# A graph kernel's edge tables moved from its first pass into LSTM pass 2, with a new load order and new orders in pass 1's last tiles

## The reference, cut to what matters

```
h = relu(adj @ (x @ Wg0 + bg0));  h = relu(adj @ (h @ Wg1 + bg1))
for p in 1..4:   # windows of p steps; the last step of each window is replaced
    h[:, last of window] = last state of LSTM_p over the window (p steps)
x = layernorm(x + h)
# graph attention over E = 256 edges (src, dst)
Xq, Xv = x @ W_lin.T, x @ W_val.T
e = sum_d a * leaky_relu(Xq[src] + Xq[dst]) + log(adj[src, dst] + 1e-8)
attn = softmax of e over the edges of one src;  Y[src] += attn * Xv[dst]
x = layernorm(x + Y @ W_out.T)
```

## Time and profile before

| | |
|---|---|
| median of 3 runs | 907.78 us (907.5 to 908.27) |
| profiled execution | 907.49 us, of which its span 905.4 us |
| TensorE busy | 873.8 us, 97% |
| VectorE busy | 696.4 us, 77% |
| ScalarE busy | 610.9 us, 67% |
| GpSimd busy | 176.9 us, 20% |
| granted TensorE clock, mean | 0.998 |

### The profile page before, as it was taken

How to read it: one execution, slowest core, us unless ns; L and a number is a source line. 1 busy time by engine, 2 the same in 40 slices (tenths; PEclk the granted TensorE clock), 3 DMA queues, 4 the chain that set the end, 5 groups by cost and what they waited for, 6 DMA issues and landing times.

```text
span 905.4 us, 15427 instructions
## 1 busy us (share of the span) xinstructions
PE 873.8 (97%) x5411; PEld 759.5 (84%) x5411; DVE 696.4 (77%) x1570; ACT 610.9 (67%) x1113; POOL 176.9 (20%) x500
## 2 busy tenths in 40 slices
PE   7999999999999999999999999999998999999796
PEld 6888888877787779999998887878887888987685
DVE  5777777777778788777787677777987887886786
ACT  2677777777767667677676666666886777776254
POOL 0000000000000000000000000113564465555665
PEclk9999999999999999999999999999999999999999
DMA  4211221001000000000000086777073010111123
GB/s 112 82 47 56 63 59 47 25 1 47 1 1 0 1 1 1 1 1 1 2 1 1 0 176 151 162 166 184 2 159 75 25 37 24 37 37 36 48 59 82
DMA packets 43275, 45.44 MB, mean 50 GB/s; under 512 B 2592, under 2 KB 40128, under 8 KB 40128
## 3 DMA queue, kind: packets, MB, share of 16 engines
q1 hardware_dynamic: 39520, 27.47, 10.5%
q0 software_dynamic: 2304, 16.78, 9.1%
q10 hardware_dynamic: 1376, 0.22, 0.1%
HBM read 19.29 MB, written 8.39 MB: 31 GB/s over the span
## 4 chain that ended last, share of the span: by engine, by line
PE 85%; DVE 8%; issue 3%; ACT 3%; DMA 1%; ACTq 0%; POOL 0%; POOLq 0%; DVEq 0%
PE psum L446 8%; PE psum L447 8%; PE psum L448 8%; PE psum L464 6%; PE psum L460 6%; PE psum L461 6%; PE psum L1174 6%; PE psum L1101 6%; PE psum L364 3%; PE psum L382 3%; PE psum L392 3%; PE psum L1185 2%; PE psum L1157 2%; PE psum L355 2%; PE psum L354 2%
## 5 line engine op out<-in xcount | busy, mean ns | idle before, releaser
L564 ACT ACTIVATE work<-psum,bias 128x512 f32<-128x512 f32 (+1 forms) x408 | 233.3, 623 | 29.1 <-PE psum L464 28.5
L446 PE MATMUL psum<-hT_hi,w_hi 128*128 128x512 f32 (+1 forms) x408 | 148.7, 365 | 3.3 <-ACT work L564 2.6
L447 PE MATMUL psum<-hT_lo,w_hi 128*128 128x512 f32 (+1 forms) x408 | 147.3, 361 | 0.0
L448 PE MATMUL psum<-hT_hi,w_lo 128*128 128x512 f32 (+1 forms) x408 | 147.2, 361 | 0.0
L548 ACT ACTIVATE work<-work 128x512 f32<-128x512 f32 (+1 forms) x112 | 63.9, 570 | 102.1 <-DVE work L819 70.8
L1009 POOL DMA_DIRECT2D hT_lo<-hT_hi x8 | 7.3, 918 | 556.1 <-DVE hT_lo L794 536.9
L828 DVE TENSOR_TENSOR work<-work 128x512 f32<-128x512 f32 (+1 forms) x111 | 67.9, 611 | 54.1 <-ACT work L548 54.1
L460 PE MATMUL psum<-hs_hi,w_hi 128*128 128x512 f32 (+1 forms) x288 | 103.8, 360 | 0.8 <-DVE hs_hi L792 0.7
L464 PE MATMUL psum<-hs_lo,w_hi 128*128 128x512 f32 (+1 forms) x288 | 104.4, 363 | 0.0
L461 PE MATMUL psum<-hs_hi,w_lo 128*128 128x512 f32 (+1 forms) x288 | 103.2, 358 | 0.0
L446 PEld LDWEIGHTS psum<-hT_hi,w_hi 128*128 128x128 f32 x408 | 76.8, 188 | 17.4 <-ACT work L564 5.4
(11 more groups left out here) (206 smaller groups left out, 1862.8 us busy)
## 6 DMA issues: line engine op xcount, KB each, us to landing
work<-x SPq DMA_DIRECT2D x32, 256.0 KB, 3.0
x_stage<-x_by_feature SPq DMA_DIRECT2D x8, 1024.0 KB, 5.6
hT_lo<-hT_hi POOLq DMA_DIRECT2D x8, 1024.0 KB, 9.7
hT_lo<-x_stage POOLq DMA_DIRECT2D x8, 1024.0 KB, 7.0
out<-x_kept SPq DMA_DIRECT2D x31, 256.0 KB, 2.3
work<-L_gnn_Wih SPq DMA_DIRECT2D x4, 256.0 KB, 3.1
work<-L_gnn_Whh SPq DMA_DIRECT2D x3, 256.0 KB, 3.0
out<-x_kept SPq DMA_DIRECT2D x2, 128.0 KB, 2.3
```

The source lines that it names most:

```text
L446: pe.matmul(out, w_hi[:, w, g, :], xh, start=True, stop=False)
L447: pe.matmul(out, w_hi[:, w, g, :], xl, start=False, stop=False)
L448: mm = pe.matmul(out, w_lo[:, w, g, :], xh, start=False, stop=(t == 0))
L564: op = act.activation(gate[s][g][:, 0:ph.width], psum[:, 4 * s + g, 0:ph.width], ACT.Tanh if g == G else ACT.Sigmoid, bias=bias[:, b:b + 1])
```

## The change: what it does

1. **Loads.** `adj` goes to ScalarE's queue as its first, with `bg0` and `Wg0`. SP issues x of tiles 0, 1, 2 at once, then the weights, and the edges' lists and `a` last. ScalarE runs a one-column copy (`first_act`) after its first three loads, and issues the other five after that.
2. **Ones multiplied at first.** TensorE makes five f32 products of the tile `ones` as soon as that is filled, before it waits for `adj`, and one more after the transposition. The `degrees` and `rank_rows` products move one slot later, the biases' transposition to slot 3.
3. **Edge tables.** They leave pass 1. On VectorE they are cut into thirteen pieces, most of them at the head of one item of pass 2 (`edge_numbers` at j = 1, `edge_keys` 3, `rank_edges` 5, `permutes` 7, `sorted_cols` 8, `sorted_rows` 12, `row_edges` 13, `edge_ends` 15, `adjacent` 16, `sames` 17, `signs` 19, `caps` 21), the last two in pass 3. TensorE makes its parts at the head of items 8, 12 and 16 of pass 2 and item 6 of pass 3, in the free F bank. The logarithm follows item 2 of pass 3.
4. **One-pass products.** `permute` and `spread` are f32r, so the four products of 256 columns are f32r products. The other sorting products stay f32.
5. **Attention weights.** Their transposition moves from slot 3 to slot 7, their centring to slot 6, their copies to slot 8.
6. **Pass 1's last tiles.** From slot 34 on ScalarE reads gate O before it makes the tanh, and VectorE makes the cell before it cuts the state of the tile before. In slot 36, TensorE makes gates I and G of pass 2's first item between gates G and O of tile 31 (`first_input`), in the idle banks of the layers.

The diff, cut to the places that matter here:

```diff
+
+    SORT_COLS, SORT_ROWS, ADJACENT = 8, 12, 16
+    LOG_AT, DIAG_AT, LOG_ROWS_AT = 2, 4, 6
...
+    permute = sb("permute", [P, EC, E], F32R)
+    spread = sb("spread", [P, 2, EC, P], F32R)
     sorted_col = sb("sorted_col", [P, EC, 2])
     adj_edge = sb("adj_edge", [P, EC])
...
 
-        sp.dma_start(adj_sb[:, :], adj).then_inc(S["adj_loaded"], 16)
         load_x(0)
-        sp.dma_start(wg0[:, :], Wg0).then_inc(S["wg0_loaded"], 16)
-        sp.dma_start(edge_row_i[:, :], src.rearrange("(a e) -> a e", a=1).broadcast_to([P, E])).then_inc(S["rows_loaded"], 16)
         load_x(1)
+        load_x(2)
         load_piece(0)
         for j, w in enumerate((W_lin, W_val, W_out)):
             sp.dma_start(w_raw[1][:, j, :], w).then_inc(raw_loaded[1], 16)
-        load_x(2)
+        sp.dma_start(edge_row_i[:, :], src.rearrange("(a e) -> a e", a=1).broadcast_to([P, E])).then_inc(S["rows_loaded"], 16)
+        for j, e in enumerate((src, dst)):
+            sp.dma_start(edge_col_i[:, j, :], e.rearrange("(c p) -> p c", p=P), allow_slow_non_contiguous=True).then_inc(S["cols_loaded"], 16)
+        sp.wait_ge(S["a_zero"], 1)
+        for h in range(HEADS):
+            sp.dma_start(T.a_wide[h * DH:(h + 1) * DH, T.a_col + h:T.a_col + h + 1], a[h].rearrange("(d o) -> d o", o=1),
+                         allow_slow_non_contiguous=True).then_inc(S["a_loaded"], 16)
         for n in range(SLOTS):
...
+        def sort_cols():
             pe.wait_ge(S["permutes"], EC)
+            for r in range(EC):
+                for c in range(EC):
+                    mm = pe.matmul(psum[:, F, 2 * r:2 * r + 2], permute[:, c, r * P:(r + 1) * P].bitcast(F32), edge_col[:, c, :],
+                                   start=(c == 0), stop=(c == EC - 1))
+            mm.then_inc(S["cols_psum"], 1)
+
+        def sort_rows():
             pe.wait_ge(S["spreads"], 2 * EC)
-            pe.wait_ge(S["degree_ready"], 2)
             for j in range(2):
...
+        def first_input(g, bank, free):
+
+            assert bank == g
+            ph = phases[1]
...
+            xh, xl = windows_at(ph, hi_bt, 0, 0, 0), windows_at(ph, lo_bt, 0, 0, 0)
+            w, out = piece_of[1, 0], psum[:, bank, 0:ph.width]
+            pe.wait_ge(S["w_lo_ready"], len(pieces))
+            pe.matmul(out, w_hi[:, w, g, :], xh, start=True, stop=False)
+            pe.matmul(out, w_hi[:, w, g, :], xl, start=False, stop=False)
+            pe.matmul(out, w_lo[:, w, g, :], xh, start=False, stop=True).then_inc(gate_psum[g], 1)
 
         def slot(n):
...
                 mm.then_inc(S["ah_psum"], 1)
+            if n - 5 == tiles - 1:
+                first_input(I, AX, S["axT_ready"])
+                first_input(G, AH, S["ahT_ready"])
             if has(n - 5):
...
+        def run_warm(count):
+
+            for _ in range(count):
+                pe.matmul(psum[:, GATE_BANK[O], 0:P], ones[:, :], ones[:, :], start=True, stop=True)
+
+        pe.wait_ge(S["consts"], 1)
+        run_warm(5)
         pe.wait_ge(S["adj_loaded"], 16)
         pe.wait_ge(S["ident_ready"], 1)
         pe.transpose(psum[:, SIDE, 0:P], adj_sb[:, :], ident[:, :]).then_inc(S["adjT_psum"], 1)
-        degrees()
+        run_warm(1)
+        pe.wait_ge(S["adjT_ready"], 1)
         for n in range(SLOTS):
             slot(n)
             if n == 0:
+                degrees()
+            elif n == 1:
                 rank_rows()
-            elif n == 1:
-                sort_edges()
-            elif n == 2:
...
+                    if ph is phases[1]:
+                        if j in (SORT_COLS, SORT_ROWS, ADJACENT):
+                            assert t == 0 and k % 2 == 0
+                            pe.wait_ge(S["gates_read"], ph.items_before + j + (CREDIT - 1))
+                        if j == SORT_COLS:
+                            sort_cols()
+                        elif j == SORT_COLS + 2:
...
     def run_scalar(act, entry):
+        act.dma_start(adj_sb[:, :], adj).then_inc(S["adj_loaded"], 16)
         act.dma_start(bg0_all[:, :], bg0.rearrange("(a h) -> a h", a=1).broadcast_to([P, P])).then_inc(S["bg0_loaded"], 16)
-        for j, e in enumerate((src, dst)):
-            act.dma_start(edge_col_i[:, j, :], e.rearrange("(c p) -> p c", p=P), allow_slow_non_contiguous=True).then_inc(S["cols_loaded"], 16)
+        act.dma_start(wg0[:, :], Wg0).then_inc(S["wg0_loaded"], 16)
...
+                ended = not has(n - 2)
+                if ended:
+                    gate_of(O, k)
...
                         tanh_of(k)
+                    if ph is phases[2] and it == 0 and k == LOG_AT:
+                        act.wait_ge(S["eps_done"], 1)
+                        act.activation(log_adj[:, :], adj_edge[:, :], ACT.Ln).then_inc(S["log_done"], 1)
...
+
+            ended = not has(n - 2)
+            if ended and has(n - 5):
+                cell_product(n - 5)
             if has(n - 6):
-                k = n - 6
...
                             entry.scale_query(dve)
+                    j = it * ph.per_iter + k
+                    if ph is phases[1]:
+                        if j == 1:
+                            edge_numbers()
+                        elif j == 3:
+                            edge_keys()
+                        elif j == 5:
+                            rank_edges()
+                        elif j == SORT_COLS - 1:
+                            permutes()
+                        elif j == SORT_COLS:
+                            sorted_cols()
...
+                        log_rows()
                     if t > 0:
                         dve.wait_ge(S["f_ready"], nf)
```

197 lines of the change are left out of this document (120 added, 77 removed).

## The result

The changed kernel takes 902.4 us (median of 5 runs, 901.25 to 903.26); the kernel before, run beside it, takes 907.78 (5 runs, 907.48 to 908.83). The ratio is 0.9941, 95% interval 0.9928 to 0.9954: faster by 0.6%. The forecast was 899.9, with a range of 896.4 to 903.8. The sign and the range hold, and the gain is 5.4 us where 7.85 were forecast.

The account below looks back on a forecast made before the run. TensorE, busy 97% of the span, was taken as the bound. Start -9.0, `log_to_rows` -0.45, weights +0.3, end of pass 1 -2.8, edge tables +4.1 sum to -7.85 from 907.49; plus 0.3 to the median: 899.9 us, range 896.4 to 903.8.

Parts of the forecast that it names:

- The start: Stretch before slot 5: new loads, ones and tables moved out start slot 5 at 20.6 instead of 29.55, -9.0 us.
- the slow work: First blocks at the start: products slow until TensorE has worked without pause; 0.2 us, or 0.9 more per first two blocks.
- The worse case for `bg1`: Rank rows at the start: taken as in time, with up to 2 us of waiting if `bg1` lands at 11.3.
- `log_to_rows` and the weights' turning: Pass 1: moving `log_to_rows` out gives 0.45 us; turning the attention's weights in slot 7 puts 0.3 back.
- The end of pass 1: Last tiles: four waits for ScalarE, 2.81 us together, mostly go by reading gate O first; -2.8, bounds -1.4 and -3.4.
- Pass 2: Edge pieces delay VectorE's chain, which TensorE pays: +1.3 us at item 8, +1.7 at items 12 to 16.
- the waits of 0.5 for the low half: Sign in pass 2: TensorE waits for `hs_lo` of items 8 and 16, about 0.5 us each.
- Pass 3: The logarithm's table loads make item 3's state 0.5 us late; with `log_rows` and diagonals 0.6, +1.1.
- A: Rival, passes 2 and 3: VectorE's pieces are hidden, only TensorE's 2.2 us is paid; 898.0 us, chance 0.20.
- C: Rival, pass 3: the logarithm's switches stall ScalarE 5.5 us instead of 2.8, the extra reaching TensorE; 902.6, chance 0.05.
- B: Rival, start: x lands late and work stays slow through two tiles, slot 5 at 24.0; 903.3 us, chance 0.20.
- D: Slower rival, passes 2 to 4: one chain, each edge piece delays it wholly, 14.1 us; 909.9 us, chance 0.04.

Follow-up runs that it names:

- `bg1` early: The kernel with the logarithm in pass 4, with `Wg1` and `bg1` issued by SyncE between x of tiles 1 and 2; 898.45 us.
- The run with the pieces behind the cell: The kernel with the ones filled up, with `sorted_cols`, `adjacent`, `log_rows` behind the item's cell and TensorE's wait for them ahead of gate F, made last; 899.99 us.
- The run with tables in pass 1: The kernel before with the new loads, ones and end of pass 1, but tables, their f32 products and attention weights at their old places; 904.85 us.
- the ones filled up: The changed kernel with seven ones instead of five ahead of `adj` and two more ahead of the degrees; 901.32 us.
- the old end of pass 1: The changed kernel with the orders of pass 1's last tiles as in the kernel before; one execution, 904.01 us.
- the logarithm as a copy: The changed kernel with `Ln` replaced by `Copy`, leaving out the logarithm and both table loads; one execution, 901.24 us.
- the f32 tables: The changed kernel with `permute` and `spread` f32 again; one execution, 903.49 us.
- the logarithm in pass 4: The kernel with the pieces behind the cell, with logarithm, diagonals and rows at items 4, 6, 8 of pass 4 instead of pass 3; 899.93 us.
- The best kernel found: The kernel with `bg1` early, with GpSimd computing the attention's first two sets of layer norm factors ahead of the addition of x; 896.64 us.

## Why the prediction was right in sign and 2.5 us too hopeful

**The start, -9.0 forecast, -6.0 measured: the step that failed.** It is the term "I put 0.2 for it", the slow work. The other terms of that step hold: x's block starts at 4.81 (forecast 5.3, so 0.5 better); the hole is 0.9 (6.6 to 7.51), where 0.75 stood, but it comes from `bg0`, not from ScalarE's copy; and from 13.07 to slot 5's block at 23.77 TensorE takes 10.70, where the forecast's 14.35, less three blocks, degrees and rank rows (3.8), leaves 10.55.

The slow work costs: the first block 0.9, the degrees 0.4 (0.85 against 0.45), the second block 0.94, the third 0.81 (10.20 to 11.91), the rank rows 0.51 (11.91 to 13.07 against 0.65): 3.56 instead of 0.2. In sum 3.36 + 0.15 + 0.15 - 0.49 = 3.17 late: slot 5 at 23.77 instead of 20.6. The forecast had set its 20.6 against 29.55, which is the start of slot 4's last product; slot 5's block stands at 29.77 in before, so 20.6 meant -9.2, and the gap is -9.2 to -6.0. (Its lower bound, 19.6, left out the 4.7 that it had named for `adjT`; and ScalarE had twelve issues ahead of its table load in before, not thirteen.)

The forecast had said what it costs "if it is not" used up, 0.9 for each of two blocks, and had counted neither the third block nor the small products. Its 0.2 took the ones to use most of the slow time up by 5.3, although its own hole of 0.75 was to stand right behind the first block. In four profiled executions with the change's ones this came out twice (fast from 4.97 and 5.41) and failed twice (12.93 in after, and 13.62). In all six with ten ones instead of six the work was fast by 6.4, and the median is 1.1 us less. So the term was right for some executions of this code and wrong for others, after's among them. What decides it is not shown, and the pauses alone do not: the executions with 4.97 and 13.62 have the same instructions, their TensorE starts x's block within 0.03 of each other (4.49 and 4.52) and neither waited for `adj`; and in all six with ten ones the work was fast before the two ones that fill the pause behind x's block. With `bg1` early as well, slot 5 starts at 20.58.

**The worse case for `bg1`** ("up to 2 us if it lands at 11.3"): in after it did not show, because the slow work brought TensorE there only at 11.91. Once the slow work went, it showed, 0.93. One delay had covered the other.

**`log_to_rows` and the weights' turning, -0.45 and +0.3**: -0.45 and +0.33.

**The end of pass 1, -2.8**: -2.72, and 2.6 with the old orders put back.

**Pass 2, +3.0** (item 8 +1.3, items 12 to 16 +1.7): +2.62 from item 2 to item 18's state part (-8.83 to -6.21), inside the 1.8 to 4.5 named beforehand. The size holds, the mechanism in part. Up to the state part that needs item 8's state it is +1.42 (-8.83 to -7.41), where 1.3 were forecast; but 0.88 of it are TensorE's own products and 0.3 the start of these products, and the chain through the piece ahead of the cell ends only 0.2 later than that. TensorE's own products in pass 2 take 1.7 (0.88, 0.47, 0.36), which the forecast had as 1.75 and had put inside VectorE's chain. The run with the pieces behind the cell took back 0.6 at item 8 and 0.7 at item 18. Not as forecast is the last part: at item 18 TensorE waits for the result of `adjacent` by itself (267.15), a wait that the change adds and that the forecast did not price; of the waits of 0.5 for the low half that it named as signs, the one at item 8 is 0.2 more than before, the one at item 16 is not there.

**Pass 3, +1.1**: +2.18 at item 8's first product, 2.3 behind it. The size is off. The stall of ScalarE is as forecast, 335.92 to 338.74, but I let it reach TensorE for 0.5; without the table loads TensorE gains 2.0. The stall does not end with item 3's state, as I had assumed. The wait of 0.63 for `log_row` at 349.29 was not priced either.

**The rivals.** A (TensorE's 2.2 alone, 898.0) falls: the edge work cost 4.8 in passes 2 and 3 (2.62 + 2.18). C (902.6) names the measured 902.4 almost to the point, and that is luck: its mechanism is absent, see below. B (the start gives less, 903.3) comes next. Half its mechanism is right: the work stays slow, and for three pieces more (third block, degrees, rank rows) than the two blocks that it counted. The other half, late x, is wrong. C (the logarithm's two switches stall ScalarE for 5.5) falls: the stall is 2.8. The Trainium skill, page "ScalarE: Activation LUTs", section "What ACT_TABLE_LOAD costs", gives a drain of about 1.38 us to each switch beside the load of 1.28; here the load at 335.92 ends at 337.20, the logarithm starts at 337.22, ends at 337.42, and the next load starts at 337.44; the activation ahead of the first load (335.42, 0.49 long) ends at 335.91. The load's length agrees, the drain is not there, and the measurement decides. D (all exposed) falls: 4.8 of the 14.1 reached the end.

**The end of the trace.** 0.5 to 0.6 us more ahead at the end than behind pass 3 came in the attention, and was not forecast. Between two of the runs with the same instructions there, that stage shifted by 1.0, so nothing is read from it.

What stays open: how much of the 6.0 us is due to the tables' move alone. The run with tables in pass 1 differs from after in their place, in the order of degrees and rank rows and in VectorE's order of `bg0` and `adjT`, and these were not run apart.

## What to carry to other kernels

Do not count on work given to TensorE to raise its clock early until several executions have shown it: with six products of ones it came out in two profiled executions of four, with ten in six of six. Then move what the faster work uncovers (here `bg1`) forward as well. A piece on an engine with slack still costs time (here 0.6 of its 0.98) where it stands ahead of the instruction that the bounding engine waits for; put it behind that one, and put the wait for it as late in the item as it can go. When a gain made early is missing at the end, look for an in-order queue that waits for transfers on the way (here GpSimd's), and take out of it what does not need those transfers.

## What the runs showed that I had not expected

The granted clock's column reads 1.00 in stretches where a block of 128-column products takes 1.84 instead of 0.9 us, about the ratio of the two levels, 1.2 and 2.4 GHz. The traces of all these kernels have no clock record in their first microseconds, and the column fills them with 1.00. The first record stands where the work gets fast: 13.94 in before, 12.93 in after, 10.79 without ones, 5.88 with the ones filled up. At the start, the length of a block is what tells the clock.

Where the slow work ends differs between executions without a reason in the code. Four kernels have the same instructions at the start (after, the old end of pass 1, the logarithm as a copy, the f32 tables): it ends at 12.93, 5.41, 13.62 and 4.97, in the last with a fall back to 0.50 from 8.38 to 11.80, and slot 5 starts at 23.77, 22.03, 23.99 and 22.78. That is as much as several of the effects studied here, and in the single run with the old end of pass 1 it covered more than half of the 2.6 us. With the ones filled up it ends between 3.92 and 6.36 in six kernels, and the times of 4 or 5 runs then lie within 0.14 to 0.96 us (2.0 in after).

Twelve transfers of 1 MB that add to a buffer, chained one by one, take from 510 to 620 us, in steps of 7.2 to 12.6 us. They follow the computation only loosely: with the logarithm in pass 4, TensorE was 1.9 us ahead, and the last of these issues left 5.3 us later (620.89 against 615.61), because waits along the chain grew; the first, ahead of the chain's second issue, was 10.50 instead of 7.09. Why they grew is not shown. The best kernel found, with all of this, takes 896.64 us, 1.2% less than before and 0.6% less than the changed kernel.
